# Slot experts: which tiles are scattered and which are placed by TensorE, with four sum buffers and blank products at the start

## Reference, cut to what matters

```python
h = silu(x[idx] @ w_gate[e]) * (x[idx] @ w_up[e])      # e = 0..63, at most 64 tokens each
contrib = (h @ w_down[e]) * weight * valid
routed = segment_sum(contrib, token, num_segments=T)
gu = x @ ws_gate_up
out = routed + (silu(gu[:, :SF]) * gu[:, SF:]) @ ws_down
```

## Time and profile before

| | us |
|---|---|
| median of 3 runs | 1397.5 (1397.26 to 1397.58) |
| the profiled execution, whole | 1397.07 |
| its span, first to last instruction | 1395.3 |
| PE busy in the span | 1111.8 (80%) |
| DVE busy | 823.7 (59%) |
| ACT busy | 546.6 (39%) |
| POOL busy | 343.3 (25%) |
| mean granted TensorE clock | 0.87 of 2.4 GHz |

### The profile page before, as it was taken

How to read it: one execution, slowest core, us unless ns; L and a number is a source line. 1 busy time by engine, 2 the same in 40 slices (tenths; PEclk the granted TensorE clock), 3 DMA queues, 4 the chain that set the end, 5 groups by cost and what they waited for, 6 DMA issues and landing times. The chain is left out here.

```text
span 1395.3 us, 31629 instructions
## 1 busy us (share of the span) xinstructions
PE 1111.8 (80%) x10680; PEld 817.0 (59%) x10680; DVE 823.7 (59%) x2873; ACT 546.6 (39%) x1175; POOL 343.3 (25%) x471
## 2 busy tenths in 40 slices
PE   8999889886887544789976856987698979789791
PEld 4655546775454531456644424553678969789791
DVE  6566163333588897745566885546853656656334
ACT  4456522454432001222222114322115757667581
POOL 3344325133100000000000015540033424424351
PEclk9999999998988557799997966999877989989896
DMA  2200646452000019238217065553902212021222
GB/s 52 53 25 3 241 171 248 159 196 67 1 3 3 4 37 374 85 82 177 38 40 257 2 201 133 145 114 124 301 21 64 56 35 59 24 65 44 50 52 62
DMA packets 112351, 135.02 MB, mean 97 GB/s; under 512 B 16795, under 2 KB 78316, under 8 KB 111539
## 3 DMA queue, kind: packets, MB, share of 16 engines
q1 hardware_dynamic: 99730, 118.48, 27.6%
q0 software_dynamic: 12464, 14.53, 4.1%
HBM read 67.13 MB, written 69.06 MB: 98 GB/s over the span
## 5 line engine op out<-in xcount | busy, mean ns | idle before, releaser
L2044 PE MATMUL m_psY<-large,m_hT 128*128 x992 | 141.5, 286 | 0.2
L2030 PE MATMUL m_psH<-m_xT,m_up 128*128 128x128 f32 x992 | 139.3, 286 | 0.0
L2030 PEld LDWEIGHTS m_psH<-m_xT,m_up 128*128 128x128 f32 x992 | 129.3, 203 | 0.0
L2044 PEld LDWEIGHTS m_psY<-large,m_hT 128*128 128x128 f32 x992 | 129.0, 194 | 0.5 <-issue 0.3
L1970 POOL DMA_INDIRECT rows<-m_ys,m_slot x93 | 90.5, 973 | 132.1 <-DVE m_slot L2238 119.7
L567 DVE TENSOR_REDUCE at_peaks<-at_ps 128x3 f32<-128x384 f32 x128 | 65.4, 551 | 47.8 <-PE at_ps L330 47.8
L2087 ACT ACTIVATE m_up<-large 128x512 f32 x124 | 78.0, 629 | 29.5 <-DVE m_valid L2141 17.2
L479 ACT ACTIVATE at_PT<-at_ps,at_bias 128x384 f32<-128x384 f32 x128 | 67.3, 577 | 50.3 <-PE at_ps L340 50.2
L1445 POOL IOTA sl_late<- 64x1024 f32 x2 | 2.0, 984 | 331.1 <-POOLq L682 331.1
L2096 ACT ACTIVATE m_hT<-m_psH 128x512 f32<-128x512 f32 x124 | 73.2, 590 | 20.6 <-PE m_psH L2030 20.4
L126 PE MATMUL ln_idle<-blank,ident 128*128 128x512 f32 x112 | 53.7, 635 | 26.2 <-PEq L883 13.5
(11 more groups left out here) (662 smaller groups left out, 2682.7 us busy)
## 6 DMA issues: line engine op xcount, KB each, us to landing
rows<-blank SPq DMA_DIRECT2D x16, 2448.0 KB, 15.2
m_xs<-rows SPq DMA_DIRECT2D x124, 76.5 KB, 1.9
pair_rows<-blank SPq DMA_DIRECT2D x1, 8320.0 KB, 25.8
large<-in_L_attn_firs SPq DMA_DIRECT2D x4, 2048.0 KB, 18.0
large<-comb_rows SPq DMA_DIRECT2D x64, 128.0 KB, 4.9
se_wu<-in_L_ffn_up SPq DMA_DIRECT2D x32, 192.0 KB, 2.6
W2T<-in_L_ffn_down_turned SPq DMA_DIRECT2D x1, 4096.0 KB, 12.6
large<-in_L_ffn_up SPq DMA_DIRECT2D x4, 1024.0 KB, 8.1
```

The lines of the kernel that those rows point to most:

```text
L2030: m = nc.tensor.matmul(psH[b][:, c * P:(c + 1) * P], up[b][:, c * P:(c + 1) * P], xT[b][:], start=True, stop=True)
L2044: m = nc.tensor.matmul(psY[b][:, 0:wide], hT[b][:, c * P:(c + 1) * P], k.W2[:, bass.ds(e + c * WIDE, wide)], start=(c == 0), stop=(c == C ...
```

## The change

Tiles with j mod 3 = 2 are placed (10 of 32), all others scattered (22). `SUMS` is 4: the scattered tiles take the buffer pairs (0, 1) and (2, 3) by turns, each pair has its own semaphore, and a scatter waits for the one before the last (`SENT[i - 2]`). `base` of every tile with j mod 3 = 1 is written again with two buffers' offset, by two more iotas on POOL. Everything that has a size of `SUMS` grows with it: the clearing, the read back (four DMAs of 1 MB) and the adds at L1761 (16 for 8). DVE makes `place` in the iteration before a placed tile, as before. PE gets `WARMING - 2` = 6 blank products ahead of tile 0.

```diff
@@ slots_stage, POOL
+            for h in range(2):
+                nc.gpsimd.iota(base[h * E2:(h + 1) * E2, 1::3], [[0, len(range(1, SLOT_TILES, 3))]], base=(h + 2) * N, ...
+            pool.wait_ge(*made.at(6))
@@ slot_experts_stage
-    stored = k.tally("stored0")
+    stored = [k.tally(f"stored{i}") for i in range(2)]
-    landed = lambda j: stored.at(16 * (j // 2 + 1))
-    by_place = lambda j: j % 2 == 1
+    by_place = lambda j: j % 3 == 2
+    PLACED = [j for j in range(SLOT_TILES) if by_place(j)]
+    SENT = [j for j in range(SLOT_TILES) if not by_place(j)]
+    landed = lambda j: stored[SENT.index(j) % 2].at(16 * (SENT.index(j) // 2 + 1))
@@ POOL
-                    if j >= 2:
-                        pool.wait_ge(*landed(j - 2))
+                    i = SENT.index(j)
+                    if i >= 2:
+                        pool.wait_ge(*landed(SENT[i - 2]))
-                        .then_inc(stored.sem, 16)
+                        .then_inc(stored[i % 2].sem, 16)
@@ SP
-            sp.wait_ge(*landed(SLOT_TILES - 2))
+            sp.wait_ge(*landed(SENT[-2]))
+            sp.wait_ge(*landed(SENT[-1]))
@@ PE
+            for i in range(WARMING - 2):
+                nc.tensor.matmul(psX[:], k.ident[:], k.blank[:, 0:512], start=True, stop=True)
@@ DVE
-                    else:
-                        if j >= 4:
-                            dve.wait_ge(*used.at(j // 2 - 1))
-                        nc.vector.tensor_scalar(place[:, j // 2 % 2, :], count[:], token[:, j + 1:j + 2], None, ALU.is_equal)\
+                    elif j + 1 in PLACED:
+                        q = PLACED.index(j + 1)
+                        if q >= 2:
+                            dve.wait_ge(*used.at(q - 1))
+                        nc.vector.tensor_scalar(place[:, q % 2, :], count[:], token[:, j + 1:j + 2], None, ALU.is_equal)\
                             .then_inc(placed.sem, 1)
@@
-SUMS = 2
+SUMS = 4
```

More of the change, by code:

```diff
@@ L1452, in _ @@
             pool.wait_ge(*made.at(4))
+            for h in range(2):
+                nc.gpsimd.iota(base[h * E2:(h + 1) * E2, 1::3], [[0, len(range(1, SLOT_TILES, 3))]], base=(h + 2) * N,
+                               channel_multiplier=0, allow_small_or_imprecise_dtypes=True).then_inc(made.sem, 1)
+            pool.wait_ge(*made.at(6))
             nc.gpsimd.iota(numbers[:], [[1, N]], base=0, channel_multiplier=0,
@@ L1538, in _ @@
             nc.vector.tensor_copy(top[:, 1, :], top[:, 0, :]).then_inc(listed.sem, 1)
-            dve.wait_ge(*made.at(5))
+            dve.wait_ge(*made.at(7))
             nc.vector.tensor_copy(count[:], numbers[:])
@@ L1548, in slots_stage @@
     w_in.close(32)
-    made.close(5)
+    made.close(7)
     for t in (up_done, silu_done, hid_done, down_done):
@@ L1659, in _ @@
                 if 0 <= j and by_place(j):
-                    pe.wait_ge(*split.at(j // 2 + 1))
-                    pe.wait_ge(*placed.at(j // 2 + 1))
+                    q = PLACED.index(j)
+                    pe.wait_ge(*split.at(q + 1))
+                    pe.wait_ge(*placed.at(q + 1))
                     for part in range(3):
                         for g in range(NBLK):
-                            i = nc.tensor.matmul(acc[:, g, :], parts[:, j // 2 % 2, part, :], place[:, j // 2 % 2, g * 512:(g + 1) * 512],
+                            i = nc.tensor.matmul(acc[:, g, :], parts[:, q % 2, part, :], place[:, q % 2, g * 512:(g + 1) * 512],
                                                  start=False, stop=True, skip_group_check=True)
@@ L1697, in _ @@
                     if j >= UNROLL:
-                        act.wait_ge(*(split.at((j - UNROLL) // 2 + 1) if by_place(j) else landed(j - UNROLL)))
+                        act.wait_ge(*(split.at(PLACED.index(j - UNROLL) + 1) if by_place(j - UNROLL)
+                                      else landed(j - UNROLL)))
                     nc.scalar.activation(ys[0:SLOTS, j % UNROLL, :], psY[0:SLOTS, 0:D], ACT.Copy,
                                          scale=xs[0:SLOTS, j % XROOM, D + 2 * j:D + 2 * j + 1]).then_inc(y_half.sem, 1)
-            act.wait_ge(*used.at(SLOT_TILES // 2))
+            act.wait_ge(*used.at(len(PLACED)))
             for g in range(NBLK):
@@ L1728, in _ @@
                     dve.wait_ge(*down_done.at(j + 1))
-                    if j >= UNROLL and not by_place(j):
+                    if j >= UNROLL and not by_place(j - UNROLL):
                         dve.wait_ge(*landed(j - UNROLL))
@@ L1734, in _ @@
                     if by_place(j):
-                        y, mine = ys[:, j % UNROLL, :], parts[:, j // 2 % 2]
-                        if j >= 4:
-                            dve.wait_ge(*used.at(j // 2 - 1))
+                        q = PLACED.index(j)
+                        y, mine = ys[:, j % UNROLL, :], parts[:, q % 2]
+                        if q >= 2:
+                            dve.wait_ge(*used.at(q - 1))
                         dve.wait_ge(*y_half.at(j + 1))
@@ L1766, in slot_experts_stage @@
         t.close(32 * SLOT_TILES // UNROLL)
-    stored.close(16 * SLOT_TILES // 2)
+    for i, t in enumerate(stored):
+        t.close(16 * len(SENT[i::2]))
     for t in returned:
@@ L1772, in slot_experts_stage @@
     for t in (placed, used, split):
-        t.close(SLOT_TILES // 2)
+        t.close(len(PLACED))
     for t in (copied, turned_back):
```

## The result

The changed kernel takes 1413.9 us (median; 1409.96 to 1414.6), the kernel before 1397.4 beside it: a ratio of 1.0113, 95% interval 1.008 to 1.0145. It is slower, as forecast, but by twice as much: 1405.4 was said, and 1411 was the upper end of the range. The profiled execution has a span of 1412.3, 17.0 more than before.

The account below looks back on a forecast made before the run. Prediction: a closed loop of waits bounds the kernel before, POOL's queue the changed rounds. 1397.1 - 8.1 (rounds) + 2.5 (start) - 2.0 (last tiles) + 5.9 (read back) = 1395.4, + 10 (clock) = 1405.4 us; own range 1401 to 1411, overall 1393 to 1411.

Parts of the forecast that it names:

- Rounds of three tiles: 24 tiles from tile 7's transpose to tile 31's: eight rounds of 8.0 us, 64.0 for 72.1, so -8.1 us.
- loop of waits: Scatter, gather behind it, PE's transpose, down product, next scatter: 7.5 us a round, below POOL's queue at 8.0.
- The queue's gap: POOL's idle time between a gather and the scatter behind it: 0.46 us taken, bounds 0.30 and 0.75.
- The clock: PE's clock falls in five of ten rounds through idle time between placements, 2.0 us each: +10 us, bounds 0 and +20.
- Rival C: PE's clock is down for most of the stage, each fall keeping it down: 1415 to 1433 us, chance 0.08.
- Rival A: PE's clock holds through the rounds: 1395.4 us, between 1393 and 1398, chance 0.27.
- Rival B: POOL's queue is quicker, gap 0.30 and gathers 0.95: rounds of 7.6 us, 1392.2 with clock up, chance 0.08.
- Rival D: Scatters in flight disturb each other and land later: 2 to 4 us more, 1398 to 1400, chance within Rival A's.
- Start: Stage's start up to tile 7: blanks delay the first scatter +1.2, first placement at lower clock +1.3: +2.5 us.
- Last tiles: Tile 31's transpose to SP's read back issue: 9.4 us in place of 11.4, so -2.0, bounds -3 and 0.
- Read back and adds: SP's issue to end of adds: twice the bytes and 16 adds, 17.5 for 11.7 us: +5.9, bounds +5.5 and +8.
- Hidden: More clearing, POOL's two iotas and two waits, six places fewer on DVE: 0 us, all off the path.

Follow-up runs that it names:

- the run with a lead of six: Changed kernel with gathers issued six tiles ahead of the scatters in place of four (AHEAD 6): ratio 0.9961 to the kernel before.
- the second trace: The changed kernel profiled once more, unaltered, on another chip: 1409.7 us in a single execution.
- the runs with a lead of five and six: Changed kernel with gathers five or six tiles ahead in place of four: 1388.6 us (five, single execution); ratio 0.9961 to the kernel before (six).
- the run with 512 columns: Changed kernel plus a PE zero product of 512 columns, added to acc, in each iteration without a placement: ratio 1.0073 to the kernel before.

## Why the prediction was wrong, step by step

**Rounds of three tiles: the step that failed.** The forecast took the queue of POOL, 8.0, as the bound, since its loop of waits gave only 7.5. That loop went from a scatter to the one gather behind it and back to a scatter three tiles on, and had neither the second scatter nor the placement in it. The change puts two scatters with a gather between them ahead of the gather of the next round: 3.58 + (1.62 + 0.30 + 0.99 + 0.30) + (1.59 + 0.30) + 3.53 for the landing = 12.2 us from T(20) to T(24), and then PE's iteration with the placement and a plain one, 5.2. Closed over six tiles it is 17.0 to 17.4 us, 8.5 to 8.7 a round and 68.1 to 69.5 for 24 tiles, where the sum has 64.0: 4 to 5.5 short, the whole miss of that row. A test on the kernel before would not have found it. There a circle goes over four tiles and holds one scatter and one placement: from T(20) at 903.08 to T(24) at 914.30 it is 11.2 us, and the forecast's own terms, 7.5 and the placement iteration of 3.88, give 11.4, 2.85 a tile for the 2.91 read from the earlier trace rows. What was missing came with the change: in the new order of POOL's queue a second scatter and its neighbour gather stand inside the circle, and the placement iteration, which the forecast kept in the circle of before, stands in it once in two rounds.

**The queue's gap.** 0.46 was the wrong choice between the bounds; 0.30 was seen (eleven gaps, 3.4 us). It hardly mattered, as POOL wasn't the bound; 7.69 for a round in the run with a lead of six shows what it would have been worth.

**The clock.** The direction was right (more idle time of PE between placements, and the clock falls), and the sum of +10 came out, in part by luck: 78.9 less 68.1 to 69.5 is 9.4 to 10.8 us (8.1 to 9.5 in the second trace), for 10. It was put together otherwise: four falls in 24 tiles at some 2.5 us (five in the second trace) instead of five in ten rounds at 2.0. And ahead of a fall PE stood 1.06 and 2.67 us for gathers 23 and 24, not 1.6 in a round whose length POOL's queue sets. As in Rival C one fall seems to bring on the next, but by another way: a slow round delays `ys`, POOL stands idle for it (4.12 ahead of scatter 18) and then issues in a burst, PE waits 2.67 for a gather, and that wait precedes the next fall. That is the order in the trace; no run tests it apart from the lead of the gathers. Rival A fell: the clock didn't hold. Rival B's gap was there, its round was not. Rival D fell by the runs with a lead of five and six.

**Start.** +2.0 for +2.5, with other parts: the blanks account for some 0.5 (26.1 without them), where 1.2 was put down to them, and the other 1.5 or so came with the rest of the change. T(0) came 7.5 behind the stage's start (845 was said, so 7.2), the first scatter 0.9 later for 1.2, and the clock was lost in the wait for gather 5, as described.

**Last tiles.** -1.5 for -2.0. The last scatter landed 957.11 - 953.85 = 3.26 after its start. Tile 30's stood 1.8 us later behind T(31) than the 3.0 worked out, because DVE splits tile 29 into its three parts (949.26 to 950.5) before it comes to `ys` of tile 30, a wait that the forecast left out; its successor followed in 1.86, not 2.06.

**Read back and adds.** +5.9 for +5.9, and +6.1 with four buffers alone.

**Hidden.** The clearing, the iotas and the waits showed no cost: the stage of the second trace begins 0.4 us earlier than before. The one wait that the line view gives to a landing, 2.3 us, stands ahead of the scatter at 945.14, whose `ys` ACT began to write only at 943.9, so it was most likely a wait for `ys` too. Six places fewer bought nothing: they shorten gathers on an engine that waited 28 us for `ys`. A gather beside the making of `place` is longer again (1.24 at 924.69 in the run with 512 columns, 0.99 elsewhere). By the Trainium skill ("SBUF — State Buffer", section "Who interferes with whom"), of a VectorE instruction in a two-port mode and GpSimd the one that issues first has their shared ports for its whole length, and the other is blocked. The trace agrees: the gather began 0.38 us behind a `place` of 0.75 and is 0.25 longer. The rule didn't decide.

**The spread.** 3.9 us of the span were the execution's own. The forecast had no term for what one execution differs from another outside the change, although its range of 18 us was wide enough for one: with it, 1405.4 + 4 to 5.5 for the loop is 1409.4 to 1410.9, and the execution of the second trace, on another chip, took 1409.7. The median of the four runs lies 3 to 4.5 us above that; only one of them was profiled, so whether the others lost it in the same place isn't known.

## What to carry to other kernels

Close a loop of waits around every engine that it passes, over as many rounds as it needs to come back to the same place. Test it on the kernel before, but don't stop there: here the forecast's terms fitted the kernel before to 2%, and failed because the change put more steps into the circle. Write down the new order of the queue and follow it to the last transfer that a waiting engine needs. Where PE waits for a transfer that was queued behind work that waits for PE, lead it by one tile more before moving work between engines; here a lead of five or six in place of four was worth more than the new share of tiles. An engine that gets work off (PE, 6 to 7 us) shortens nothing when the engine that takes it is as long, and less matmul work between waits can cost the clock.

## What the runs showed that I had not expected

- A program can settle in a cycle of two unlike rounds: 7.1 to 7.5 and 11.4 to 13.6 us by turns, in four traces of three kernels. In three of them it goes over all 24 tiles; in the second trace of the changed kernel two like rounds of 9.5 and 10.0 us stand ahead of it. In the first trace the falls of the clock are 20.5 us apart.
- A lead of one gather more turned 78 us into 61 (one execution), and left the clock at 1.00 but for 3.4 us.
- The kernel before lost the clock in some executions and not in others (low 3.4, 0 and, with four buffers, 10.2 us), and ranged over 20 us in 27 of them, though one profile beside three equal times looked firm to 0.2%.
- POOL issued an adding scatter 0.30 us after the gather ahead of it, as it does a gather; the 0.46 of the scatter in the earlier trace rows wasn't seen again in this burst.
